# Result additions, row loads and the order of small steps in an attention and expert-layer kernel

## The reference

```
du   = zX*lap_x(x) + zY*lap_y(x) + zR*x*(1-x)        # reflecting borders
qkv  = layernorm(du) @ in_proj.T + b                 # causal, 16 heads of 16, over 16 positions
x1   = du + attention(q, k, v) @ out_proj.T + b
h    = layernorm(x1)
gates= the 2 largest of softmax(h @ router.T)        # not renormalized
y    = sum over the 2 experts of  gate * gelu(h @ w1[e]) @ w2[e]     # 256 -> 512 -> 256
out  = x + x1 + y
```

## Time and profile before

| | us |
|---|---|
| median of 3 runs (805.82 to 810.01) | 807.31 |
| profiled execution | 808.75 |
| its span | 807.0 |
| busy PE / DVE / ACT / POOL | 631.2 / 435.5 / 357.2 / 454.5 |
| mean clock granted to PE, share of full | 0.881 |

### The profile page before, as it was taken

The page is one execution under the profiler, slowest core; times in us unless marked ns, Lnnn a source line. Parts: engine busy times, 40 slices in busy tenths (PEclk is TensorE's granted clock), DMA queues, the critical chain, the costliest instruction groups (busy, mean ns, idle before and its releaser), DMA issues.

```text
span 807.0 us, 9988 instructions
## 1 busy us (share of the span) xinstructions
PE 631.2 (78%) x2640; PEld 414.5 (51%) x2640; DVE 435.5 (54%) x1009; ACT 357.2 (44%) x817; POOL 454.5 (56%) x518
## 2 busy tenths in 40 slices
PE   1358788585568589979798779998799599999990
PEld 1124455344435456645465556766566365665660
DVE  1136789999599945456766668989514000111110
ACT  3343333232132247757465546654456255444430
POOL 4666677758844734687585555763644533333332
PEclk9977877788586889979799789999899699999996
DMA  3335654312321122333223213242444333434332
GB/s 95 104 128 176 205 151 127 89 31 80 86 51 31 46 47 51 85 81 71 64 49 79 42 32 60 56 74 39 73 77 81 80 54 61 60 54 63 57 48 26
DMA packets 51098, 59.82 MB, mean 74 GB/s; under 512 B 6938, under 2 KB 46627, under 8 KB 50980
## 3 DMA queue, kind: packets, MB, share of 16 engines
q0 software_dynamic: 18288, 23.28, 18.4%
q1 hardware_dynamic: 32756, 35.90, 15.4%
HBM read 35.89 MB, written 27.46 MB: 79 GB/s over the span
## 4 chain that ended last, share of the span: by engine, by line
DMA 30%; PE 20%; DVE 19%; POOL 14%; issue 10%; SPq 3%; ACT 3%; POOLq 0%; ACTq 0%; DVEq 0%
DMA out_dram<-y,xin 20%; DMA xud<-in_x_dram 9%; DVE qk_prod L797 4%; PE b_y L932 4%; DVE sc L805 4%; PE b_qk L1009 4%; DVE pv_prod L863 3%; POOL xs_d L386 3%; PE b_h L917 3%; PE b_at L1053 2%; PE b_at L993 2%; PE b_v L1009 2%; POOL rstd L378 2%; POOL du L370 1%; POOL xs_d L393 1%
## 5 line engine op out<-in xcount | busy, mean ns | idle before, releaser
L412 POOL DMA_INDIRECT out_dram<-y,xin x71 | 116.1, 1635 | 151.6 <-DMA out_dram<-y,xin 124.0
L932 PE MATMUL b_y<-w_s,hm_hmT 128*128 x568 | 140.2, 391 | 10.2 <-ACT y L511 9.4
L917 PE MATMUL b_h<-w_s,xT 128*128 x284 | 134.5, 596 | 1.6 <-ACT xT L472 1.6
L932 PEld LDWEIGHTS b_y<-w_s,hm_hmT 128*128 128x128 f32 x568 | 105.7, 196 | 24.7 <-issue 12.5
L1053 PE MATMUL b_at<-ident,pv_prod 128*128 128x128 f32 x544 | 83.6, 309 | 39.4 <-DVE pv_prod L863 39.4
L1053 PEld LDWEIGHTS b_at<-ident,pv_prod 128*128 128x128 f32 x544 | 74.3, 165 | 44.0 <-issue 38.8
L644 DVE TENSOR_SCALAR y<-b_y,xin,live 128x256 f32<-128x256 f32 x24 | 13.1, 544 | 155.0 <-PE b_y L932 155.0
L863 DVE TENSOR_TENSOR pv_prod<-kv,pr 128x1024 f32<-128x1024 f32 (+2 forms) x80 | 84.3, 1098 | 13.9 <-PE b_at L1053 13.8
L797 DVE TENSOR_TENSOR qk_prod<-q,kv 128x1024 f32<-128x1024 f32 (+2 forms) x80 | 90.3, 1152 | 0.8
L1009 PE MATMUL b_qk<-wqkv,hT 128*128 128x512 f32 x128 | 86.1, 808 | 0.0
L805 DVE TENSOR_REDUCE sc<-qk_prod 128x64 f32<-128x1024 f32 (+2 forms) x80 | 82.1, 1051 | 0.3
(11 more groups left out here) (160 smaller groups left out, 1022.3 us busy)
## 6 DMA issues: line engine op xcount, KB each, us to landing
xin<-xs_d SPq DMA_DIRECT2D x71, 132.5 KB, 2.2
w_s<-in_L_ffn_w_dram SPq DMA_DIRECT2D x16, 512.0 KB, 8.3
xp<-in_x_dram SPq DMA_DIRECT2D x32, 128.0 KB
xud<-in_x_dram SPq DMA_DIRECT2D x32, 128.0 KB
out_dram<-x POOLq DMA_DIRECT2D x32, 128.0 KB, 3.3
xud<-in_x_dram SPq DMA_DIRECT2D x32, 127.0 KB
out_dram<-y,xin POOLq DMA_INDIRECT x71
xs_d<-ring,slot_row POOLq DMA_INDIRECT x64
```

Source lines behind the costliest of these rows:

```text
L412: pool.indirect_dma_start(out_rows, bass.IndirectOffsetOnAxis(ap=xin[:, j % NX, H:H + 1].bitcast(U32), axis=0), y[:, j % NY, :], None, com ...
L917: mm = pe.matmul(b_h[:, :], xT[:, k * P:(k + 1) * P], w1_s[:, bass.ds(e * (HC * F) + k * F, F)], start=(k == 0), stop=(k == HC - 1))
L932: mm = pe.matmul(b_y[:, 0:H], hmT[:, k * P:(k + 1) * P], w2_s[:, bass.ds(e * (FC * H) + k * H, H)], start=(k == 0), stop=(k == FC - 1))
```

## The change

It does four things. (1) Additions: `y_added` becomes two semaphores, for even and odd tiles. From tile LEFT[0] on, POOL reads from a new table `tabw` how far the addition before must have come: where the first row of tile j is exactly 128 behind that of tile j - 1, which is the same expert continued, tile j waits only for the addition of tile j - 2; elsewhere for that of j - 1, as before. POOL then runs a one-column addition, whose result is not used, behind this wait. DVE makes `tabw` in `route_b`. (2) The 127-row loads become one of 126 rows and one of 1 row; each load has five pieces. (3) For g < 0 POOL's deviation of the first layer norm stands before `neighbours`, and for later steps where it was. (4) WANT has one slot, not two, in each of steps 32, 33 and 34, so LEFT is tiles 30 to 70; and the last group's five steps of scatters each have one addition behind them.

```
-    CAP = G * P + P
+    CAP = G * P + 2 * P
+        iota_w = sb("iota_w", [P, 2 * (ALL // 2 + 1)], I32)      # 0, 0, 16, 16, 32, 32, ...
...
-        WANT = [0] * 10 + [1, 1, 1, 2, 2, 2, 2] + [2, 1, 1, 1, 1, 1, 2, 2] + [2, 2, 2, 2, 2, 2, 2, 2, 2, 2]
+        WANT = [0] * 10 + [1, 1, 1, 2, 2, 2, 2] + [2, 1, 1, 1, 1, 1, 2, 2] + [2, 2, 2, 2, 2, 2, 2] + [1, 1, 1]
...
+        def added_to(j):
+            return y_added[j % 2], 16 * (j // 2 + 1)
...
                 if c == 0:
-                    sp.dma_start(up[0:1, :], x[p, 1:2, :]).then_inc(x_in[i], 16)
-                    sp.dma_start(up[1:P, :], x[p, 0:P - 1, :]).then_inc(x_in[i], 16)
+                    sp.dma_start(first[0], first[1]).then_inc(x_in[i], 16)
+                    sp.dma_start(up[1:P - 1, :], x[p, 0:P - 2, :]).then_inc(x_in[i], 16)
+                    sp.dma_start(up[P - 1:P, :], x[p, P - 2:P - 1, :]).then_inc(x_in[i], 16)
                     sp.dma_start(dn, x[p, 1:P + 1, :]).then_inc(x_in[i], 16)
                 else:
                     sp.dma_start(up, x[p, c * P - 1:(c + 1) * P - 1, :]).then_inc(x_in[i], 16)
-                    sp.dma_start(dn[0:P - 1, :], x[p, c * P + 1:(c + 1) * P, :]).then_inc(x_in[i], 16)
-                    sp.dma_start(dn[P - 1:P, :], x[p, B - 2:B - 1, :]).then_inc(x_in[i], 16)
+                    sp.dma_start(dn[0:P - 2, :], x[p, c * P + 1:(c + 1) * P - 1, :]).then_inc(x_in[i], 16)
+                    sp.dma_start(dn[P - 2:P - 1, :], x[p, (c + 1) * P - 1:(c + 1) * P, :]).then_inc(x_in[i], 16)
+                    sp.dma_start(last[0], last[1]).then_inc(x_in[i], 16)
...
-                if j >= 1:
-                    pool.wait_ge(s["y_added"], 16 * j)
+                if j >= LEFT[0]:
+                    behind = pool.value_load(tabw[0:1, j:j + 1], min_val=16, max_val=16 * ALL)
+                    pool.wait_ge(y_added[(j - 1) % 2], behind)
+                    pool.tensor_tensor(passed[:, j:j + 1], power[:, :], power[:, :], ALU.add)
+                elif j >= 1:
+                    pool.wait_ge(*added_to(j - 1))
+                if j >= 2:
+                    pool.wait_ge(*added_to(j - 2))
...
+                if g < 0 <= g + 3:
+                    deviation(g + 3, 0)
                 if g + AHEAD + 1 < G:
                     neighbours(g + AHEAD + 1)
-                if 0 <= g + 3 < G:
+                if 0 <= g < G - 3:
                     deviation(g + 3, 0)
...
             for g in GROUPS[NG - 1]:
                 scatter(g)
+                add_y(left.pop(0))
...
+                if r >= 1:
+                    a, b = FIRST[r], FIRST[r + 1]
+                    step = tick(dve.tensor_tensor(apart[:, 0:m], tabr[:, a:b], tabr[:, a - 1:b - 1], ALU.subtract))
+                    need(step)
+                    step = tick(dve.tensor_scalar(apart[:, 0:m], apart[:, 0:m], P, -16, ALU.is_equal, ALU.mult))
+                    need(step)
+                    dve.tensor_tensor(tabw[:, a:b], apart[:, 0:m], iota_w[:, a + 1:b + 1], ALU.add).then_inc(s["tab_ready"], 1)
+                else:
+                    dve.tensor_copy(tabw[:, 0:m], iota_w[:, 1:m + 1]).then_inc(s["tab_ready"], 1)
```

More of the change, by code:

```diff
@@ L127, in adaln_moe_block @@
         tabr = sb("tabr", [P, ALL], I32)
+        tabw = sb("tabw", [P, ALL], I32)
+        passed = sb("passed", [P, ALL])
+        apart = sb("apart", [P, TMAX], I32)
         live = sb("live", [P, TMAX])
@@ L144, in adaln_moe_block @@
             rt_sub rt_exp rt_m rt_cum rt_cum_sb slots_ready tab_ready pre_ready
-            x_tr xT_sb h_ready gelu_done hT2_ready hmT_sb y_ready y_sb y_added pre_done
+            x_tr xT_sb h_ready gelu_done hT2_ready hmT_sb y_ready y_sb pre_done
             dve_chain pool_chain""".split()
         s = {n: sem(n) for n in names}
-        x_in = pair("x_in")
+        x_in, y_added = pair("x_in"), pair("y_added")
         x1_added = [sem(f"x1_added{i}") for i in range(4)]
@@ L243, in load @@
                 up, dn = xud[:, i, 0, :], xud[:, i, 1, :]
+                first = up[0:1, :], x[p, 1:2, :]
+                last = dn[P - 1:P, :], x[p, B - 2:B - 1, :]
                 if c == 0:
-                    sp.dma_start(up[0:1, :], x[p, 1:2, :]).then_inc(x_in[i], 16)
-                    sp.dma_start(up[1:P, :], x[p, 0:P - 1, :]).then_inc(x_in[i], 16)
+                    sp.dma_start(first[0], first[1]).then_inc(x_in[i], 16)
+                    sp.dma_start(up[1:P - 1, :], x[p, 0:P - 2, :]).then_inc(x_in[i], 16)
+                    sp.dma_start(up[P - 1:P, :], x[p, P - 2:P - 1, :]).then_inc(x_in[i], 16)
                     sp.dma_start(dn, x[p, 1:P + 1, :]).then_inc(x_in[i], 16)
@@ L280, in tile_in @@
                 if j >= NX:
-                    sp.wait_ge(s["y_added"], 16 * (j - NX + 1))
+                    sp.wait_ge(*added_to(j - NX))
                 row = sp.value_load(tabr[0:1, j:j + 1], min_val=0, max_val=E * CAP - P)
@@ L316, in _ @@
                 sp.wait_ge(x1_added[i], 16 * (G // 4))
-            sp.wait_ge(s["y_added"], 16 * ALL)
+            for j in (ALL - 2, ALL - 1):
+                sp.wait_ge(*added_to(j))
         @block.gpsimd
@@ L350, in later_constants @@
                                       channel_multiplier=1)]
+                links_of.append(pool.iota(iota_w[:, :].rearrange("p (a b) -> p a b", b=2), [[16, ALL // 2 + 1], [0, 2]],
+                                          base=0, channel_multiplier=0))
                 link(links_of[-1])
@@ L358, in neighbours @@
                 i = g % 2
-                pool.wait_ge(x_in[i], 64 * (g // 2 + 1))
+                pool.wait_ge(x_in[i], 80 * (g // 2 + 1))
                 link(pool.tensor_copy(xp[:, i, 0:H + 2:H + 1], xp[:, i, 2:H:H - 3]))
@@ L409, in add_y @@
                         pool.wait_ge(x1_added[i], 16 * len([g for g in range(ENDS[group_of(j)]) if g % 4 == i]))
-                if j >= 1:
-                    pool.wait_ge(s["y_added"], 16 * j)
+                if j >= LEFT[0]:
[6 more added lines that the diff above has]
+                    pool.wait_ge(*added_to(j - 2))
                 pool.indirect_dma_start(out_rows, bass.IndirectOffsetOnAxis(ap=xin[:, j % NX, H:H + 1].bitcast(U32), axis=0),
-                                        y[:, j % NY, :], None, compute_op=ALU.add).then_inc(s["y_added"], 16)
+                                        y[:, j % NY, :], None, compute_op=ALU.add).then_inc(y_added[j % 2], 16)
             def scatter_at(g, n):
@@ L461, in scale @@
                     act.wait_ge(s["x1_ready"], g - DU + 1)
-                act.wait_ge(x_in[i], 64 * (g // 2 + 1))
+                act.wait_ge(x_in[i], 80 * (g // 2 + 1))
                 act.activation(du[:, g % DU, :], xp[:, i, 1:H + 1], ACT.Identity, bias=alpha[:, 0, p:p + 1],
@@ L509, in result @@
                 if j >= NY:
-                    act.wait_ge(s["y_added"], 16 * (j - NY + 1))
+                    act.wait_ge(*added_to(j - NY))
                 act.activation(y[:, j % NY, :], b_y[:, 0:H], ACT.Copy,
@@ L642, in result @@
                 dve.wait_ge(s["y_ready"], j + 1)
-                dve.wait_ge(s["y_added"], 16 * (j - NY + 1))
+                dve.wait_ge(*added_to(j - NY))
                 dve.tensor_scalar(y[:, j % NY, :], b_y[:, 0:H], xin[:, j % NX, bass.ds(e + (H + 1), 1)],
@@ L751, in route_b @@
                 if not final:
-                    dve.tensor_scalar(row, tf[:, 1, 0:m], s8[:, 0:1], None, ALU.add)
+                    rows_made = tick(dve.tensor_scalar(row, tf[:, 1, 0:m], s8[:, 0:1], None, ALU.add))
                 else:
@@ L761, in route_b @@
                     link(dve.tensor_tensor(tf[:, 2, 0:m], tf[:, 2, 0:m], tf[:, 1, 0:m], ALU.min))
-                    dve.tensor_copy(row, tf[:, 2, 0:m])
+                    rows_made = tick(dve.tensor_copy(row, tf[:, 2, 0:m]))
                     link(dve.tensor_tensor(tf[:, 1, 0:m], tf[:, 1, 0:m], tf[:, 2, 0:m], ALU.subtract))
@@ L765, in route_b @@
                 need(te)
-                dve.tensor_copy(tab[:, FIRST[r]:FIRST[r + 1]], tf[:, 0, 0:m]).then_inc(s["tab_ready"], 1)
+                te = tick(dve.tensor_copy(tab[:, FIRST[r]:FIRST[r + 1]], tf[:, 0, 0:m]))
+                need(rows_made)
+                if r >= 1:
[7 more added lines that the diff above has]
+                    dve.tensor_copy(tabw[:, 0:m], iota_w[:, 1:m + 1]).then_inc(s["tab_ready"], 1)
             for g in range(-AHEAD, G + 3):
```

## The result

The changed kernel takes 746.65 us (median of four runs, 746.07 to 748.15) against 808.35 us for the kernel before in the same comparison (805.82 to 810.01): a ratio of 0.9242, with the interval 0.9212 to 0.9272, or 61.7 us less. The forecast was 756, with a range from 736 to 780. The profiled execution has a span of 746.4 us (807.0 before) and a mean clock of 0.902 (0.881). (A slip ahead of the prediction: the title of Rows 4 names wrong tiles. Its rows are the copies of tiles 2, 3, 7, 12 and 31.)

A forecast was written before the change was run, and what follows sets the result against it. It took late loads (127-row pieces on one DMA engine) and, in the tail, additions each waiting for the one before as the bound: 808.75 - 25 - 9 - 19 + 2 = 757.75, less 1.44 for the median, 756 us; range 736 to 780.

The forecast's parts named there:

- The 127-row piece: In each xin load: 127 rows run on one DMA engine of 16, and what comes behind waits; 5.7 us.
- Rival A: Loads: 126 rows are no better than 127, only tail and table gains remain; 790 us, chance 0.10.
- Early, -25 us: Before 121 us: load waits of 32.6 us go, 2.5 and 5 come back; range -12 to -33.
- 8.6 us for an iteration without loads: Five iterations from 67.86 to 121.02 us, less POOL's 10.1 us of load waits: 8.6 us each.
- rival B: Early stretch: TensorE's half clock and weights' traffic replace the load waits; -12 early, -5 late, 773 us, chance 0.20.
- Late, -9 us: Two late loads at 435.26 and 460.01 us shorten from 9.59 and 8.74 to about 2.6 each; range -3 to -13.
- The deviation, +2.5: In the three steps g < 0, the moved deviation no longer fills POOL's wait for ScalarE; 2.5 us, bounds 0 and 2.5.
- VectorE's table, +2: Three more chained VectorE operations for each of seven groups; some 4 us, half on its chain: +2 (0 to 4).
- The tail, -19 us: Additions 30 to 70 take 178 us instead of 193.6, gain 15.6; addition 30 comes 3 us sooner besides.
- Bounds of the extra: 0 and 2.16: Waiting tail additions: range for the added instruction's extra time, taken as 0.35 us, making 4.92 from 4.57.
- rival C: Whole kernel: everything is hidden; -33 early, -13 late, TensorE-bound tail -34; 727 us, chance 0.12.
- Rival D: Tail: register wait and instruction stand before each addition at 2.16 us, no pair saves anything; 854 us, chance 0.03.

The follow-up runs named there:

- 113-row run: Changed kernel with the 127 rows cut into 113 and 14 instead of 126 and 1; 775.01 us, ratio 0.9584.

## Why the prediction was right

**Right in direction and range, 9 us too high. The mechanism of the loads held; that of the tail held in part, with the cost of a waiting addition wrong in its sign. Up to addition 30 the gain is 31.0 us where its terms gave 35, and behind it 29.6 where they gave 15.6. The first miss (4 us too much) hides part of the second (14 us too little), and that is luck.**

*The 127-row piece (right).* POOL's waits for loads are 4.4 us (forecast: under 8), no share of 0.07 was left in the stretches looked at, and the early and late terms were forecast at 25 + 9 = 34 (36.6 without the deviation's 2.5); the loads alone gave 32.6. Rival A fell with this, and the 113-row run shows that the number of rows did it.

*Early, -25 us (too much).* At tile 12 the gain is 21.1 us (copy at 99.87, forecast near 96), at tile 29 it is 18.2. The step that was off is the 8.6 us for an iteration without loads: from tile 7 to 12 they take 10.0 ((99.87 - 49.88)/5; 10.6 before). In these steps ScalarE waited 28.2 us for b_v, and the DMA share rose from 0.59 to 0.65. So rival B's mechanism is there: of the 10.1 us of waits that these five lost, 3.1 became gain (18.0 us at tile 7, 21.1 at tile 12). I had priced this give-back at 5 us for the whole start; these five tiles alone gave back 7. Another 3 us go between tiles 12 and 29, where I had the gain carried through: it is 19.7 at tile 15, 18.4 from tile 22 to 27 (tiles 14, with 25.1, and 28, with 16.8, stand out alone). VectorE is busy 158.09 of 174 us in most of that stretch, so a shift should have held; what takes the 3 us stays open. B's early gain of 12 was too small because the tiles up to 7 kept what they won, and its 773 also had the forecast's tail.

*Late, -9 us (right, a little small).* The copy of tile 29 in the kernel before:

```profile
418.36 0.20 POOL L360 COPY xp<-xp 128x2 f32<-128x2 f32 x1
```

From tile 29 (18.2 us ahead) to tile 31 (28.6) the gain is 10.4. The two idles are 1.23 and 3.15 us, under 4 as forecast.

*The deviation, +2.5, and VectorE's table, +2.* The first is 2.6 us at tile 4 and nothing in the time. The table was not measured alone; addition 30 comes at 573.80, where the forecast's own terms gave 569.8 (604.79 - 25 - 9 + 2 - 3).

*The tail, -19 us (the mis-sized term).* Forecast 178 us from addition 30 to 70, measured 164.0. By its own terms:

| | forecast | measured |
|---|---|---|
| an addition that waits | 28 x 4.92 | 28 x 4.37 (3 at 4.56, 25 at 4.34) |
| one that continues | 10 x 2.9 | 10 x 3.26 |
| 31 and 33, with scatters | 2 x 2.9 + 5 | 4.60 + 4.57 |
| sum | 177.6 | 164.1 |

The waiting addition is the one that counts: 28 x 0.55 = 15.4 us. I took the 4.57 of the old kernel (165.30/36 is in truth 4.59) as fixed, 1.54 of POOL and 3.0 of landing, and added 0.35 for a new instruction. In truth 0.75 us of the 3.0 were no landing but the time from the landing to the DMA's start. Of these the change took 0.41 away, its new instruction included: its read of `tabw` stands behind the wait for the data, the added instruction behind the wait for the predecessor, and the DMA behind one that has long been met. "Bounds of the extra: 0 and 2.16" left out a gain; the run in which every addition waits puts it at 4.24 - 4.59 = -0.35. A continuing tile takes 3.26 rather than 2.9; where two follow each other (37 and 38) the second takes 3.86, near TensorE's 4.1 us, which I read as data that isn't ready sooner.

The prediction named 4.9 us as the sign of its own tail, and that sign failed. The tail is rival C's in size: -29.6 us, and with the 2.4 us between tile 31's copy and addition 30 (28.6 to 31.0) -32, where C had -34. C as a whole (727) was wrong for its loads, which gave less than all their waits. What the tail's gain is made of, by experiments: pairs 11.2 us, additions between scatters 7.7, the form of the wait about 12 (measured in the kernel before), slots nothing: 31 against 29.6. These are not independent, since each of them runs into TensorE's pace, so that the sum fits so well shows little; what the form of the wait is worth inside the changed kernel was not run.

*Rival D* (POOL's register read and instruction make it slower) fell twice: additions are closer together, and the instruction added to the kernel before cost nothing, 1.0013.

## What to carry to other kernels

Look at the number of rows of every DMA: where it is a prime, as 127 and 113 here, and the DMA share falls to one engine's while it runs, split off a row. On a chain of dependent DMAs read the time from landing to the next start apart from the landing itself, and see that the instruction that waits last carries one wait only; in the kernel before that was worth 12 us, as much as two in flight in the changed one. When a serial chain is shortened, take the next engine's pace as the answer first (here TensorE's 4.1 us a tile): the details of the chain only count down to it.

## What the runs showed of the hardware that was not expected

- A POOL DMA with two waits ahead of it starts 0.75 us after the landing that it waits for; with one wait 0.27 us; behind a compute instruction that waits, 0.34 us (0.19 + 0.15), but 0.79 (0.02 + 0.02 + 0.10 + 0.19 + 0.46) where that compute instruction has both waits ahead of it.
- Two accumulating DMAs of 128 rows in flight don't slow each other where it can be seen: the second starts 1.96 us behind the first (571.84 and 573.80) and takes 1.55 us of POOL, as each does alone. By the times of the trace's semaphores additions 36 and 37 (600.88 and 602.84) land 3.82 and 3.85 us behind their starts, as one alone does (3.7 to 3.9). The prediction had 0.6 us more.
- A compute instruction that POOL runs right behind a DMA instruction is shown at 0.78 instead of 0.19 us (572.85), overlapping the DMA's own 1.55; I read it as a span, not as work.
- A slow DMA also holds what is behind it: with the 127-row pieces gone the 512 KB loads of `w_s` landed in 4.6 us instead of 8.3 (4.3 with the loads changed alone, 8.5 with the old loads in the changed kernel).
